# Sandwich layer on eight cores: the class part of the attention output is added in PSUM by TensorE, and VectorE gates the sum in one pass

## The chip, the cores and the metric

The kernel runs on the 8 cores of one Trainium2 chip. Each core computes 2048 of the 16384 tokens (2 sequences of 8192, four cores to a sequence) and loads 1536 tokens ahead of them as a halo. The metric is the device time in microseconds of the slowest core; lower is better. The cores exchange nothing.

## The reference

`x` has shape (2, 8192, 1024), with 16 heads of 64 columns. The layer is attention over 44 fixed offsets, gated, followed by a linear layer with a factored weight:

```python
# x = x + LN(attn(LN(x)));  x = x + LN(ffn(LN(x)))
OFFSETS = 0..32, 48, 64, 96, 128, 192, 256, 384, 512, 768, 1024, 1536
q, k, v = split(x @ qkv_w.T + qkv_b)                       # heads of 64
logit_o[n] = q[n].k[n-o] / 8 * (1 + q[n].scale_embed[o]) + pos_bias[o]
p = softmax over the 44 offsets (offsets beyond the start masked)
out[n] = sum_o p_o[n] * v[n-o];  out *= if_gain
gate = sigmoid(x @ gate_w.T + gate_b)
attn = (out * gate) @ out_w.T + out_b
ffn(x) = x @ W.T, W (1024 x 1024) built from G1_R, G2_R, G1_I, G2_I
```

## The kernel before

Offsets 0 to 32 and 48 are handled for blocks of 128 neighbouring tokens (the local part: "l"). The ten others offsets are handled for classes of tokens 32 apart (the class part: "c"). The last phase, which the change touches, starts when both parts have their softmax weights in two DRAM images (`plimg`, `pcimg`).

Before the last phase, `class_pv` has computed P.V of the class part for all tokens: 16 units, each evicted from PSUM by VectorE (L654, with the v bias added) into the tile `rk` at `CF`. It lies there feature-major as `[oc][class][token of the class]`, so that neighbouring tokens are 64 elements apart. The rest of `rk` holds the raw probabilities (`PR`), the sorted ones (`PH`) and v (`VB`).

The last phase is a software pipeline over 16 tiles of 128 tokens, written out by hand: step `s` (20 of them) issues parts of four tiles. In the order of the code, which is the order on each engine's queue (the tile in brackets):

1. SyncE loads the raw probabilities of tile s+3; TensorE transposes half of the sorted probabilities of tile s+1 (`p_turn`, L613) into bank 4, and ScalarE evicts them (L375); GpSimd sorts half of those of tile s+2 (`p_sort`, L376).
2. `d_fin1(s-3)`: VectorE takes the statistics of the second linear layer's result (L262, L263, L264), ScalarE the square root (L880).
3. `d_pv(s)`: 32 small matmuls of P.V of the local part (`pv_unit`, L627) into banks 5 and 6.
4. `d_merge(s)`: VectorE adds banks 5 and 6 and the class part, permuted back to token order, into the f16 tile `AT` (L818). It frees the banks.
5. `d_fin2(s-3)`: three operations of one element per partition on VectorE (L883, L884, L886).
6. `d_gate(s)`: VectorE multiplies `AT` by the gate (in `ry`) into `GA` (L826).
7. `d_op(s-1, 0)`: first half of the output projection on TensorE (`proj`: one matmul for the bias, L831, eight of 128x512, L834).
8. `d_tr(s-2)`: TensorE transposes the normalized tile (L864), ScalarE evicts it (L868).
9. The second half of `p_turn` (s+1) and `p_sort` (s+2), as in 1.
10. `d_fo(s-3)`: ScalarE normalizes the result of the second linear layer (L894, two halves), which frees the banks of `d_ffn`.
11. `d_op(s-1, 1)`, then `d_ln(s-1)`: VectorE statistics (L262, L263), residual (L852 twice), statistics again, with two square roots on ScalarE (L848, L856), and the normalization to f16 on ScalarE (L859).
12. Gate chunks (`g_next(3)`) as long as any are left, which is in the first steps only.
13. `d_ffn(s-2)`: the second linear layer, two times `proj`. It rotates through the same four banks as `d_op`, so that its banks are the ones that `d_fo(s-3)` frees.
14. `d_out(s-3)`: GpSimd adds (L902), SyncE stores.

Each engine takes its queue in order; a wait holds all that is behind it.

Of the kernel before, what the change touches and what calls it, by code (L numbers as in the profile page):

```python
# [12 lines left out]
ALU = mybir.AluOpType  # L13
# [3 lines left out]
TOK, HALO, TOT = 2048, 1536, 3584  # L17
NG = TOT // 512
NQ = TOK // 128
NU = 16  # L20
# [23 lines left out]
class Queues:  # L44
# [6 lines left out]
    def op(self, eng, fn, *waits, done=True):  # L51
        tok = None
        if done:
            self.count[eng] += 1
            tok = (eng, self.count[eng])
        self.q[eng].append((fn, waits, tok, 1))
        return tok
# [31 lines left out]
def sv(h, off, *dims, p0=0, np_=128):  # L89

    pitch = h.shape[1]
    return bass.AP(h, p0 * pitch + off, [[pitch, np_]] + [list(d) for d in dims])


def build_program():
# [28 lines left out]
    op, dma = qs_.op, qs_.dma  # L124

    def sb(name, cols, dtype=F16):
        return es.enter_context(nc.sbuf_tensor(name, [128, cols], dtype))

    rk = sb("rk", 8 * TOT)
    rq = sb("rq", 8 * TOK)  # L130
    ry = sb("ry", 5 * 4096)
    rw0, rw1, rw2 = sb("rw0", 8192), sb("rw1", 8192), sb("rw2", 8192)
# [4 lines left out]
    idb = sb("idb", 128)  # L137
# [6 lines left out]
    ps = es.enter_context(nc.psum_tensor("ps", [128, 4096], F32))  # L144
# [4 lines left out]
    bank = [None] * 8  # L149
# [57 lines left out]
    for name in ("plimg", "pcimg"):  # L207
        o = 0
        while o < PIMG:
            n = min(128 * 4096, PIMG - o) // 128  # L210
# [215 lines left out]
    for n, (chunk, g, oc) in enumerate(work):  # L426
        tt = 4 + n // 2
# [42 lines left out]
    s1done, pdone, scat = {}, {}, {}  # L470
# [106 lines left out]
    CF = 0  # L577
# [7 lines left out]
    def raw_load(U, *waits):  # L585
        s, kind, idx = U % 2, "cl"[U // NU], U % NU
        img = t["plimg"] if kind == "l" else t["pcimg"]
        for half in range(2):
            raw[U] = dma("sync", f"bp{s}", sv(rk, PR[s], [1, ROW], p0=half * 64, np_=64),
                         bass.AP(img, (idx * 128 + half * 64) * SKEW, [[ROW, 64], [1, ROW]]), *prfree[s], *waits)  # L590

    def v_load(U):
        s, kind, idx = U % 3, "cl"[U // NU], U % NU
        for half in range(2):
            if kind == "l":
                src = bass.AP(t["vimg"], (HALO + idx * 128 + half * 64 - 48) * D, [[D, WK], [1, D]])
            else:
                src = bass.AP(t["vimg"], (2 * idx + half) * D, [[32 * D, WK], [1, D]])
            vld[U] = dma("sync", f"bv{s}", sv(rk, VB[s] + half * 1024, [1, 1024], np_=WK), src, vbfree[s],
                         *(vdone[tt] for tt in range(NG * 4)))  # L600

    def p_sort(U, hh, eng):

        dst = sv(rk, PH + hh * 8 * WK, [WK, 8], [1, WK])
        src = sv(rk, PR[U % 2] + hh * 8, [1, 8], [16, WK])
        pcp[U, hh] = evict(eng, dst, src, raw[U], phfree[hh])
        if hh == 1:
            prfree[U % 2] = (pcp[U, 0], pcp[U, 1])

    def p_turn(U, hh, b, eng):  # L610

        for h in range(8):
            tp = op("tensor", lambda e, h=h: e.transpose(  # L613
                bass.AP(ph, b * 1024 + h * 128, [[8192, WK], [1, 128]]),
                sv(rk, PH + (hh * 8 + h) * WK, [1, WK]), idb[:]), pcp[U, hh], bank[b], done=(h == 7))
        phfree[hh] = tp
        bank[b] = ptt[U, hh] = evict(eng, PT[U % 2][0:WK, hh * 1024:(hh + 1) * 1024],
                                     bass.AP(ph, b * 1024, [[8192, WK], [1, 1024]]), tp, ptfree[U % 2])

    def pv_unit(U, b):  # L620

        s = U % 3
        for half in range(2):
            for hp in range(8):
                for r in range(2):
                    h = 2 * hp + r
                    mm = op("tensor", lambda e, h=h, hp=hp, r=r, half=half: e.matmul(  # L627
                        ps[r * 64:(r + 1) * 64, b * 512 + hp * 128 + half * 64:b * 512 + hp * 128 + half * 64 + 64],
                        sv(rk, VB[s] + half * 1024 + h * 64, [1, 64], np_=WK),
                        PT[U % 2][0:WK, h * 128 + half * 64:h * 128 + half * 64 + 64],  # L630
                        start=True, stop=True, tile_position=(0, r * 64)),
                        ptt[U, 0], ptt[U, 1], vld[U], bank[b], bank[b + 1], done=(hp == 7 and r == 1))
        vbfree[s] = ptfree[U % 2] = mm
        return mm
# [10 lines left out]
    cpart = {}  # L645
# [11 lines left out]
    gtok, thfree, gn = {}, [None, None], [0]  # L657
# [67 lines left out]
    for s in range(NB):  # L725
# [34 lines left out]
        else:  # L760
# [8 lines left out]
            U = w + 3  # L769
# [18 lines left out]
    smlast = pdone[NU - 1]  # L788


    FO = [rx[:, i * 1024:(i + 1) * 1024] for i in range(2)]
    AT = [rw1[:, i * 1024:(i + 1) * 1024] for i in range(2)]
    GA = [rw1[:, (2 + i) * 1024:(3 + i) * 1024] for i in range(2)]
    X2 = [rw1[:, (4 + i) * 1024:(5 + i) * 1024] for i in range(2)]
    XT = [rw1[:, (6 + i) * 1024:(7 + i) * 1024] for i in range(2)]
# [2 lines left out]
    pvm, gat, opm, x1t, c1t, x2t, x2f, ffm, aggt, xtt = ({} for _ in range(10))  # L798
# [12 lines left out]
    def d_pv(tt):  # L811
        pvm[tt] = pv_unit(NU + tt, 5)

    def d_merge(tt):
        src = sv(ps, 5 * 512, [128, 8], [32, 4], [1, 32])
        cin = sv(rk, CF + 4 * tt, [TOK, 8], [1, 4], [64, 32])
        at = AT[tt % 2].rearrange("p (a i c) -> p a i c", a=8, i=4)
        bank[5] = bank[6] = mrg[tt] = op("vector", lambda e: e.tensor_tensor(at, src, cin, ALU.add),  # L818
                                         pvm[tt], cpart[NU - 1], smlast)

    def d_gate(tt):
        g = 3 + tt // 4
        gsrc = sv(ry, gslot[g] * 4096 + (tt % 4) * 128, [512, 8], [1, 128])
        a2 = AT[tt % 2].rearrange("p (a n) -> p a n", a=8)
        go = GA[tt % 2].rearrange("p (a n) -> p a n", a=8)
        gat[tt] = op("vector", lambda e: e.tensor_tensor(go, a2, gsrc, ALU.mult), mrg[tt], gtok[g, 7], opm.get(tt - 2))  # L826

    def proj(src, w, wrow, half, *waits):
        b = pj_bank()
# [9 lines left out]
    def d_op(tt, half):  # L839
        opb[tt, half], opm[tt] = proj(GA[tt % 2], wo_, obr, half, gat[tt], wol)  # L840
# [21 lines left out]
    def d_tr(tt):  # L862
        for c in range(8):
            tp = op("tensor", lambda e, c=c: e.transpose(ph[:, 7 * 1024 + c * 128:7 * 1024 + (c + 1) * 128],  # L864
                                                         X2[tt % 2][:, c * 128:(c + 1) * 128], idb[:]),
                    x2t[tt], bank[7], done=(c == 7))
        x2f[tt] = tp
        bank[7] = xtt[tt] = op("scalar", lambda e: e.copy(XT[tt % 2], ph[:, 7168:8192]), tp, ffm.get(tt - 2))  # L868

    def d_ffn(tt):  # L870
        for half in range(2):
            ffb[tt, half], ffm[tt] = proj(XT[tt % 2], wbig, fbr, half, xtt[tt], wbl)
# [4 lines left out]
    def d_fin1(tt):  # L877
        src = ff_src(tt)
        a = stats(src[0], src[1], 32, ffm[tt])
        aggt[tt] = op("scalar", lambda e: e.activation(sc(46), sc(45), AF.Sqrt, bias=epsc), a)  # L880

    def d_fin2(tt):
        r = op("vector", lambda e: e.reciprocal(sc(46), sc(46)), aggt[tt])  # L883
        m = op("vector", lambda e: e.scalar_tensor_tensor(  # L884
            sc(47), sc(44), sc(46), sc(80 + tt % 4), ALU.mult, ALU.add), r)
        m = op("vector", lambda e: e.tensor_scalar(sc(47), sc(47), -1.0, None, ALU.mult), m)  # L886
        fom[tt] = m
# [6 lines left out]
                "scalar", lambda e, fo=fo, h=h: e.activation(fo, src[h], AF.Identity, bias=sc(47), scale=sc(46)),  # L894
                m, fofree[tt % 2])

    fofree, fot, mrg, fom = [pdone[NU - 1]] * 2, {}, {}, {}

    def d_out(tt):
        X = XS[tt % 4]  # L900
# [9 lines left out]
    for s in range(NQ + 4):  # L910
        old, tr, pj = (s - 3 if 0 <= s - 3 < NQ else None, s - 2 if 0 <= s - 2 < NQ else None,
                       s - 1 if 0 <= s - 1 < NQ else None)
        if s + 3 < NQ:
            raw_load(NU + s + 3)
        if s + 1 < NQ:
            p_turn(NU + s + 1, 0, 4, "scalar")
        if s + 2 < NQ:
            p_sort(NU + s + 2, 0, "gpsimd")
        if old is not None:
            d_fin1(old)  # L920
        if s < NQ:
            d_pv(s)
            if s + 3 < NQ:
                v_load(NU + s + 3)
            d_merge(s)
        if old is not None:
            d_fin2(old)
        if s < NQ:
            d_gate(s)
        if pj is not None:  # L930
            d_op(pj, 0)
        if tr is not None:
            d_tr(tr)
        if s + 1 < NQ:
            p_turn(NU + s + 1, 1, 4, "scalar")
        if s + 2 < NQ:
            p_sort(NU + s + 2, 1, "gpsimd")
        if old is not None:
            d_fo(old)
        if pj is not None:  # L940
            d_op(pj, 1)
        if pj is not None:
            d_ln(pj)
        g_next(3)
        if tr is not None:
            d_ffn(tr)
        if old is not None:
            d_out(old)
        if s >= 3:
            x_again(s + 1)  # L950
# [95 lines left out]
```

How the kernel before makes its waits and increments, by code:

```python
                def body(e, ops=self.q[eng]):  # L69
                    seen = {}
                    for fn, waits, tok, amount in ops:
                        for w in waits:
                            if w is not None and seen.get(w[0], 0) < w[1]:
                                e.wait_ge(sems[w[0]], w[1])
                                seen[w[0]] = w[1]
                        if fn is None:
                            continue
                        ins = fn(e)
                        if tok is not None:
                            ins.then_inc(sems[tok[0]], amount)
```

## Time and profile before

| | us |
|---|---|
| median of 3 runs | 731.53 (728.51 to 776.9) |
| the profiled execution | 731.03 |
| its span on the slowest core (core 0) | 729.1 |
| spans of the other cores | 719.3 to 728.6 |
| busy: TensorE, VectorE | 600.9 (82%), 431.9 (59%) |
| busy: ScalarE, GpSimd | 342.0 (47%), 272.9 (37%) |

The profiled execution took 1.9 us more than its span, before the first and after the last instruction. The shares are means over phases with different limits. The last phase is the stretch from about 498 us to the end.

### The profile page before, as it was taken

How to read it: one execution, taken by the hardware profiler on the slowest of the kernel's cores; microseconds unless marked ns; L12 is line 12 of the kernel's file. 1: busy time of each engine (PE TensorE's matmuls, PEld its weight loads, DVE VectorE, ACT ScalarE, POOL GpSimd, SP SyncE). 2: the span in 40 equal slices, each digit the busy share in tenths (PEclk: the TensorE clock that was granted, in tenths of full speed). 3: DMA queues.
4: the chain of work that ended last, by engine and by line, in shares of the span. 5: the costliest groups of instructions: out<-in, count | busy, mean ns of one | idle time of the engine just before them, and what ended most of it. 6: DMA issues, size and time to landing. Idle time of an engine off the chain costs nothing.

```text
span 729.1 us, 15108 instructions; the slowest of 8 cores (719.3 to 729.1 us)
## 1 busy us (share of the span) xinstructions
PE 600.9 (82%) x5408; PEld 312.8 (43%) x5408; DVE 431.9 (59%) x772; ACT 342.0 (47%) x480; POOL 272.9 (37%) x282
## 2 busy tenths in 40 slices
PE   1899969999989999999993496738788888888864
PEld 0444434444434555555541364535344444444431
DVE  4455555322232377788825367545458888888872
ACT  3566654333323655556531362624554545454532
POOL 3088888300000324332242445603424544445120
PEclk9999989999999999999996799857899999999996
DMA  8948997556575687898774988599314545553311
GB/s 211 237 151 224 281 272 249 181 178 204 127 147 161 186 204 209 202 245 207 184 173 75 164 205 208 151 247 248 89 51 127 172 146 170 150 167 106 116 58 58
DMA packets 73977, 126.49 MB, mean 173 GB/s; under 512 B 31116, under 2 KB 34316, under 8 KB 73392
## 3 DMA queue, kind: packets, MB, share of 16 engines
q1 hardware_dynamic: 51136, 71.06, 36.6%
q0 software_dynamic: 8608, 24.47, 17.1%
q10 hardware_dynamic: 14160, 30.00, 11.5%
q8 instruction: 44, 0.72, 0.4%
q14 instruction: 29, 0.24, 0.1%
HBM read 85.39 MB, written 50.59 MB: 187 GB/s over the span
## 4 chain that ended last, share of the span: by engine, by line
PE 46%; DVE 20%; DMA 9%; issue 8%; POOL 8%; ACT 5%; SPq 2%; DVEq 1%; ACTq 0%; POOLq 0%
PE ps L318 17%; PE ps L347 14%; PE ps L481 4%; DVE stt L262 4%; DVE stt L263 4%; PE ps L834 3%; DVE rq L852 3%; POOL rq L236 2%; DVE stt L884 2%; PE ps L499 2%; POOL rq L238 2%; SPq L62 2%; PE ps L613 2%; DMA simg<-rs 2%; DMA rk<-plimg 2%
## 5 line engine op out<-in xcount | busy, mean ns | idle before, releaser
L318 PE MATMUL ps<-ry,rw 128*128 128x512 f16 x832 | 194.6, 387 | 23.4 <-ACT rx L664 12.0
L318 PEld LDWEIGHTS ps<-ry,rw 128*128 128x128 f16 x832 | 79.2, 100 | 117.5 <-issue 33.2
L376 DVE CAST rs<-ps 128x896 f16<-128x896 f32 x32 | 34.7, 1090 | 81.1 <-PE ps L395 74.7
L613 PE MATMUL ps<-idb,rk 128*112 128x128 f16 x512 | 42.4, 236 | 41.8 <-DVE rk L376 25.1
L376 POOL COPY rk<-rk 128x896 f16<-128x896 f16 x28 | 50.3, 1804 | 70.2 <-PE ps L613 67.1
L347 PE MATMUL ps<-rw,ry 128*128 128x512 f16 x320 | 75.5, 380 | 0.0
L667 POOL TENSOR_SCALAR ry<-rx,cst 128x512 f16<-128x512 f32 x32 | 35.1, 1101 | 81.7 <-ACT rx L664 81.7
L834 PE MATMUL ps<-rw 128*128 128x512 f16 x256 | 63.0, 391 | 0.0
L834 PE MATMUL ps<-rq,rw 128*128 128x512 f16 x256 | 62.2, 387 | 0.0
L376 DVE COPY rk<-rk 128x896 f16<-128x896 f16 x36 | 35.5, 1027 | 43.0 <-DMA rk<-pcimg 22.3
L613 PEld LDWEIGHTS ps<-idb,rk 128*112 128x112 f16 x512 | 38.5, 144 | 51.8 <-issue 47.1
L352 ACT CAST rv<-ps 128x512 f16<-128x512 f32 x56 | 32.9, 587 | 55.7 <-PE ps L347 45.9
L327 ACT ACTIVATE rk<-ps,cst 128x512 f16<-128x512 f32 x56 | 38.1, 680 | 29.4 <-PE ps L318 29.3
L902 POOL TENSOR_TENSOR rq<-rq,rx 128x1024 f32<-128x1024 f32 x14 | 32.9, 2350 | 47.6 <-ACT rx L894 45.6
L62 POOL DMA_DIRECT2D rw<-cimg x32 | 16.7, 528 | 73.7 <-DMA cimg<-rs 73.5
L347 PEld LDWEIGHTS ps<-rw,ry 128*128 128x128 f16 x320 | 28.3, 98 | 36.7 <-issue 7.2
L236 POOL TENSOR_TENSOR rq<-rq 128x512 f32<-128x512 f32 x32 | 33.9, 1060 | 23.5 <-DMA rq<-g 20.0
L375 ACT COPY rv<-ps 112x1024 f16<-112x1024 f16 x32 | 31.4, 1013 | 23.4 <-PE ps L613 23.4
L334 ACT ACTIVATE rq<-ps,cst 128x512 f16<-128x512 f32 x32 | 21.7, 684 | 41.2 <-PE ps L318 34.9
L831 PE MATMUL ps<-rt,sel 128*128 128x512 f16 x64 | 25.1, 392 | 19.4 <-ACT rx L894 15.8
L664 ACT ACTIVATE rx<-ps,cst 128x512 f32<-128x512 f32 x32 | 21.7, 687 | 39.1 <-POOL ry L667 20.2
L834 PEld LDWEIGHTS ps<-rw 128*128 128x128 f16 x256 | 25.6, 100 | 30.5 <-issue 3.6
(109 smaller groups left out, 1024.6 us busy)
## 6 DMA issues: line engine op xcount, KB each, us to landing
rk<-vimg SPq DMA_DIRECT2D x64, 224.0 KB, 5.4
rx<-xs SPq DMA_DIRECT2D x18, 512.0 KB, 9.7
rq<-xs SPq DMA_DIRECT2D x16, 512.0 KB, 5.0
out<-rq SPq DMA_DIRECT2D x16, 512.0 KB, 2.7
plimg<-zt ACTq DMA_DIRECT2D x7, 1024.0 KB, 19.6
simg<-rs SPq DMA_DIRECT2D x32, 224.0 KB, 2.9
pcimg<-zt ACTq DMA_DIRECT2D x7, 1024.0 KB, 4.7
vimg<-rv ACTq DMA_DIRECT2D x28, 256.0 KB, 3.6
```

The costliest lines, as they stand in the source:

```text
L62: self.q[eng].append((lambda e: e.dma_start(out=out, in_=in_), waits, tok, 16))
L236: tk = op("gpsimd", lambda e, o_=dst, a_=a, b_=b: e.tensor_tensor(o_, a_, b_, ALU.mult), *gts[ri], tk)
L318: mm = op("tensor", lambda e, ic=ic, wof=wof: e.matmul(ps[:, b * 512:(b + 1) * 512], w[:, wof:wof + 128], yt[:, yo + ic * 512:yo + (ic + 1 ...
L327: kev[g, oc] = op("scalar", lambda e: e.activation(rk[:, oc * TOT + g * 512:oc * TOT + (g + 1) * 512], src, AF.Identity, bias=kbc[:, oc:oc ...
L347: mm = op("tensor", lambda e, ic=ic, yo=yo: e.matmul(src, yt[:, yo:yo + 128], rw0[:, half * 4096 + ic * 512:half * 4096 + (ic + 1) * 512], ...
L352: bank[b] = op("scalar", lambda e: e.copy(dst, src), mm, vst[s])
L375: return op("scalar", lambda e: e.copy(dst, src), *waits)
L376: return op(eng, lambda e: e.tensor_copy(dst, src), *waits)
L613: tp = op("tensor", lambda e, h=h: e.transpose(bass.AP(ph, b * 1024 + h * 128, [[8192, WK], [1, 128]]), sv(rk, PH + (hh * 8 + h) * WK, [1, ...
L667: gtok[g, oc] = thfree[s] = op("gpsimd", lambda e: e.tensor_scalar(dst, TH[s], hifg[:, oc:oc + 1], hifg[:, oc:oc + 1], ALU.mult, ALU.add), ...
L834: mm = op("tensor", lambda e, ic=ic: e.matmul(dst, src[:, ic * 128:(ic + 1) * 128], w[:, ic * 1024 + half * 512:ic * 1024 + (half + 1) * 512],
L902: lambda e: e.tensor_tensor(X, X, FO[tt % 2], ALU.add), fot[tt], x2t[tt])
```

## The change

For the tiles of the last phase, `pv_unit` first issues two identity matmuls (128x512, f16), one for each of the banks 5 and 6. They put the class part there in token order: the moving operand reads runs of 4 neighbouring elements of `rk`, the output is written 32 elements (128 bytes) apart. They start the accumulation, and the 32 matmuls of P.V add to it. `d_merge` and the tile `AT` go. `d_gate` multiplies the banks by the gate, straight from PSUM, and it frees the banks now, later in VectorE's order than `d_merge` did.

```diff
     def pv_unit(U, b):
         s = U % 3
+        if U >= NU:
+            for q in range(2):
+                op("tensor", lambda e, q=q: e.matmul(
+                    sv(ps, (b + q) * 512, [128, 4], [1, 32], [32, 4]), idb[:],
+                    sv(rk, CF + 4 * q * TOK + 4 * (U - NU), [TOK, 4], [64, 32], [1, 4]), start=True, stop=False),
+                    cpart[NU - 1], bank[b], bank[b + 1], done=False)
         for half in range(2):
...
-                        start=True, stop=True, tile_position=(0, r * 64)),
+                        start=(U < NU), stop=(U < NU or (half == 1 and hp % 4 == 3)), tile_position=(0, r * 64)),
...
-    AT = [rw1[:, i * 1024:(i + 1) * 1024] for i in range(2)]
...
-    def d_merge(tt):
-        src = sv(ps, 5 * 512, [128, 8], [32, 4], [1, 32])
-        cin = sv(rk, CF + 4 * tt, [TOK, 8], [1, 4], [64, 32])
-        at = AT[tt % 2].rearrange("p (a i c) -> p a i c", a=8, i=4)
-        bank[5] = bank[6] = mrg[tt] = op("vector", lambda e: e.tensor_tensor(at, src, cin, ALU.add),
-                                         pvm[tt], cpart[NU - 1], smlast)
-
     def d_gate(tt):
         g = 3 + tt // 4
+        src = sv(ps, 5 * 512, [128, 8], [1, 128])
         gsrc = sv(ry, gslot[g] * 4096 + (tt % 4) * 128, [512, 8], [1, 128])
-        a2 = AT[tt % 2].rearrange("p (a n) -> p a n", a=8)
         go = GA[tt % 2].rearrange("p (a n) -> p a n", a=8)
-        gat[tt] = op("vector", lambda e: e.tensor_tensor(go, a2, gsrc, ALU.mult), mrg[tt], gtok[g, 7], opm.get(tt - 2))
+        bank[5] = bank[6] = gat[tt] = op("vector", lambda e: e.tensor_tensor(go, src, gsrc, ALU.mult),
+                                         pvm[tt], gtok[g, 7], opm.get(tt - 2), smlast)
...
             d_pv(s)
             if s + 3 < NQ:
                 v_load(NU + s + 3)
-            d_merge(s)
```

## Rows read from the trace of the kernel before

**Rows 1.** Timeline of VectorE, core 0: start, length, engine, line, operation, tiles, shape.

```profile
616.86 1.89 DVE L818 TENSOR_TENSOR rw<-ps,rk 128x1024 f16<-128x1024 f32 x1
...
618.92 1.45 DVE L884 SCALAR_TENSOR_TENSOR stt<-stt 128x1 f32<-128x1 f32 x1
...
620.55 0.68 DVE L826 TENSOR_TENSOR rw<-rw,ry 128x1024 f16<-128x1024 f16 x1
621.15 0.69 DVE L262 BATCH_NORM_STATS2 stt<-ps 128x6 f32<-128x512 f32 x1
```

**Rows 2.** Timeline of VectorE: starts of `d_ln`; brackets: idle before, releaser.

```profile
547.61 0.69 DVE L262 BATCH_NORM_STATS2 stt<-ps 128x6 f32<-128x512 f32 x1
...
670.15 0.69 DVE L262 BATCH_NORM_STATS2 stt<-ps 128x6 f32<-128x512 f32 x1
...
681.71 0.70 DVE L262 BATCH_NORM_STATS2 stt<-ps 128x6 f32<-128x512 f32 x1 [0.47 <-PE ps L834]
...
692.73 0.69 DVE L262 BATCH_NORM_STATS2 stt<-ps 128x6 f32<-128x512 f32 x1
...
703.38 0.70 DVE L262 BATCH_NORM_STATS2 stt<-ps 128x6 f32<-128x512 f32 x1 [1.38 <-PE ps L834]
```

**Rows 3.** Timeline of ScalarE, the same step.

```profile
615.52 1.24 ACT L859 ACTIVATE rw<-rq,stt 128x1024 f16<-128x1024 f32 x1 [0.68 <-DVE stt L858]
616.66 0.99 ACT L375 COPY rv<-ps 112x1024 f16<-112x1024 f16 x1
617.56 0.29 ACT L880 ACTIVATE stt<-stt 128x1 f32<-128x1 f32 x1
...
618.65 1.02 ACT L375 COPY rv<-ps 112x1024 f16<-112x1024 f16 x1
620.79 1.45 ACT L894 ACTIVATE rx<-ps,stt 128x512 f32<-128x512 f32 x2 [1.12 <-DVE stt L886]
```

**Rows 4.** Timeline of TensorE, the same step, and one row of a later step.

```profile
617.80 0.62 PE L613 MATMUL ps<-idb,rk 128*112 128x128 f16 x8 [0.29 <-ACT rv L375]
...
618.48 1.89 PE L834 MATMUL ps<-rq,rw 128*128 128x512 f16 x8
621.71 0.38 PE L831 MATMUL ps<-rt,sel 128*128 128x512 f16 x1 [1.34 <-ACT rx L894]
...
625.59 0.61 PE L613 MATMUL ps<-idb,rk 128*112 128x128 f16 x8
...
626.76 0.39 PE L831 MATMUL ps<-rt,sel 128*128 128x512 f16 x1
...
679.72 1.89 PE L834 MATMUL ps<-rq,rw 128*128 128x512 f16 x8
```

**Rows 5.** Timeline of GpSimd, the same step.

```profile
618.56 1.80 POOL L376 COPY rk<-rk 128x896 f16<-128x896 f16 x1 [2.70 <-PE ps L613]
```

**Rows 6.** Lines L884 and L818: duration ns min/median/max, first and last start.

```profile
L884 DVE SCALAR_TENSOR_TENSOR stt<-stt x16: 219/1450/1742, 545.1 to 722.7; 128x1 f32<-128x1 f32 x16
...
L818 DVE TENSOR_TENSOR rw<-ps,rk x16: 1877/1894/1952, 499.5 to 689.7; 128x1024 f16<-128x1024 f32 x16
```

**Rows 7.** Groups by line and shape: VectorE reads PSUM without gaps (`class_pv`).

```profile
L654 DVE TENSOR_TENSOR rk<-ps,cst 128x1024 f16<-128x1024 f32 x16 | 19.4, 1215 | 0.0
```

**Rows 8.** Lines L395 (moving operand without gaps) and L481 (64 bytes apart): ns min/median/max.

```profile
L395 PE MATMUL ps<-rk,rq x512: 206/209/301, 113.8 to 228.8; 64*64 64x112 f16 x171
...
L481 PE MATMUL ps<-rk,rq x512: 363/384/481, 230.7 to 358.7; 64*64 64x112 f16 x171
```

**Rows 9.** Timeline of TensorE, first steps of the last phase.

```profile
498.24 1.06 PE L627 MATMUL ps<-rv,rk 112*64 112x64 f16 x32
499.55 1.07 PE L613 MATMUL ps<-idb,rk 128*112 128x128 f16 x8 [0.26 <-ACT rs L375]
...
506.32 0.69 PE L627 MATMUL ps<-rs,rk 112*64 112x64 f16 x32
...
525.49 1.07 PE L613 MATMUL ps<-idb,rk 128*112 128x128 f16 x8 [3.84 <-ACT rs L375]
```

More of the change, by code:

```diff
@@ L895, in d_fo @@
                 m, fofree[tt % 2])
-    fofree, fot, mrg, fom = [pdone[NU - 1]] * 2, {}, {}, {}
+    fofree, fot, fom = [pdone[NU - 1]] * 2, {}, {}
     def d_out(tt):
```

## The prediction, made before the changed kernel was run

> **What bounds the kernel now.** The page's busy shares say little: VectorE has 59% of the span, but only the last phase is touched. I read the chain that ended last there and then each engine's timeline. From 547.61 us on, `d_ln` starts at even distances: ten periods to 670.15, so 12.25 us each [rows 2]. In these steps its first operation at 621.15 has no idle time before it; it starts when L826 is through [rows 1, 2]. VectorE's queue sets the pace, while TensorE waits 1.34 us before L831 for the evictions L894 [rows 4]. VectorE's work in a period holds one oddity: L884 works on one element per partition and takes 1.45 us, in its shortest case 0.22 [rows 1, 6]. It starts at 618.92 and ends at 620.37; GpSimd's sort copy runs from 618.56 to 620.36 [rows 1, 5]. So L884 stands behind that copy.
>
> The next thing to read is what is late when VectorE isn't. Between 670.15 and 681.71 the period was 11.56 us, and there `d_ln` did wait 0.47 us, for TensorE [rows 2]. GpSimd had no more to sort in that step, L884 was short. The circle behind it, from the steady step: `d_ln` starts at T; L859 starts 6.61 later (615.52 against 621.15 less a period of 12.25); ScalarE then evicts the first transposes (L375), TensorE does the second (617.80), and the projection's eight matmuls start at 618.48, 2.96 after L859 [rows 3, 4]; VectorE takes them up 1.99 after their start (679.72 to 681.71) [rows 2, 4]. 6.61 + 2.96 + 1.99 = 11.56. No step of this circle is touched by the change. In the steady step the same sum gives 620.47 for what starts at 621.15: only **0.68 us** of a period hangs on VectorE's queue.
>
> **Part 1, merge and gate become one.** Removed: 1.89 (L818) and 0.68 (L826) [rows 1]. Added: one pass over 1024 elements that reads PSUM without gaps. The nearest row is L654, 1.22 us for the same size [rows 7]; the other end is 1.9, what L818 takes with gaps in both inputs [rows 6]. I take 1.22: of the two inputs neither has gaps now inside 128 elements. Busy time saved: 1.35 us.
>
> **Part 2, L884 moves ahead of the sort copy.** Without the merge, `d_fin2` waits for the root L880. Count from L859's start: L880 starts at 2.04, `d_ln`'s successor statistics being done earlier; root 0.29, one short VectorE operation and two hand-overs of about 0.1 (an estimate from the 0.22 of the shortest L884) bring L884 to about 2.7, its end to 2.9. The second transposes start at 2.28 and the sort copy at 3.04 [rows 3 to 6]. So L884 is short, and another 1.2 us go. Then the gate starts at about 3.1 and ends at 4.3; `d_ln` is due at 4.95. VectorE is no longer late, with 0.6 us to spare; a gate of 1.9 us would end at 5.0 and cost next to nothing in steady steps.
>
> The Trainium skill (SBUF — State Buffer, Who interferes with whom) says that a VectorE instruction with two SBUF inputs contends with a GpSimd instruction that reads SBUF, the later one blocks fully, and one with at most one SBUF input doesn't contend. The trace agrees for L884 (1.45 beside the copy, 0.22 without). By the rule the new gate, with one input in PSUM, is safe beside the copy though the copy runs during all of it, and L826 was not; were it wrong the sum would be that of the second rival.
>
> **Part 3, two identity matmuls of 512 columns on TensorE.** No row writes PSUM with gaps. Lower end: a 512-column matmul takes 0.215 (eight of them and the bias 1.94, half of the 3.88 from 621.71 to 625.59) [rows 4], so 0.43 for two. Upper end: L481 reads its 112 columns with 64-byte gaps and takes 384 ns against L395's 209, 1.56 ns more per column [rows 8]; on top of 0.42 that is 1.0 us for 512 columns and 2.03 for two. Less than 0.43 is excluded, since the columns must stream. I take 0.43, since the shape is that of L831 and L834 and the reads are runs of four; both ends stay.
>
> Is it hidden? TensorE's work in a period is 3.88 (second layer), 1.17 (transposes and P.V), 1.94 (projection), twice 0.46 (617.80 to 618.48 less one matmul) and 1.94 again, 9.85 in all [rows 4]. Now from T: L859 of the step before the next starts at 6.61, the second evict of L375 at 9.75, L894 behind it at 10.7 (earlier than now, since L884 is), the second layer 0.92 later at 11.6; transposes and P.V follow at 15.5, the projection at 16.7, the two blocks of transposes at 18.6 and 19.1, and the eight matmuls could start at 19.8. The circle wants them at 11.56 + 6.61 + 2.96 = 21.1. So **1.3 us of slack** cover the identity matmuls; at 2.03 they cost 0.7 a period, which is just what the circle gave. If that cover were gone they would cost 0.43 a step.
>
> The Trainium skill (Advanced Engine Details and Errata, PSUM Cachelines) speaks against this part: any access pattern of PSUM with gaps significantly slows matmuls, two neighbouring elements should be contiguous. It names no factor, and no matmul of this trace shows it. At half speed it would be 0.86 for two, still inside the slack, and the sum would be 0.4 higher from the first steps alone.
>
> **Part 4, banks 5 and 6 come free later.** They are freed by the gate at about T + 10.9 instead of the merge; the next identity matmuls come at T + 16. Cost nothing; the cover is 5 us. The added wait on the class part has been met since before the phase, and P.V accumulates at the same rate as L834 does.
>
> **Part 5, the first steps, where nothing hides it.** P.V of tile 0 runs before the clock has risen (1.06 against 0.69 us) [rows 9]; there the two cost twice 0.43, less the 0.26 that the next transposes wait anyway: 0.6. P.V of tile 1 at 506.32 lies on the chain, back to back with its neighbours: 0.43. In the step of tile 3 (541 to 548 us) the first L884, 545.1, waits for a double sort copy, 1.74 us [rows 6]; its root is late because ScalarE loads a table, so it stays behind the copy. The gate that follows it is on the chain and is 0.54 longer than L826: 0.54. Sum: +1.6.
>
> **The sum.** Ten periods at 0.69: −6.9. The period 681.71 to 692.73 (11.02) shrinks to that of 692.73 to 703.38 (10.65), where there is no merge: −0.4 [rows 2]. First steps: +1.6. In all −5.7, so 731.03 − 5.7 = 725.3. The profiled execution is 0.5 under the median, well inside the spread of the runs, so I give **725.5**.
>
> **The rivals.** *First, the clock.* At 525.49 TensorE has waited 3.84 us and takes 1.07 for what takes 0.61 at full clock [rows 4, 9]. The identity matmuls fill 0.43 of this wait. If the clock then stays up, transposes and projection run 0.46 + 1.94 sooner: 723. Against it: 3.4 us of waiting remain.
>
> *Second, the new order on VectorE meets the copy after all; slower.* L884 starts 0.3 us ahead of the sort copy by the sum in part 2, and this is the point from which it decides: if L884 comes at or behind 3.04 after L859, it waits for the copy's end at 4.84, and the gate, now 1.22 instead of 0.68, ends near 6.15 where `d_ln` is due at 4.95. The period is then 11.56 + 1.2 = 12.76, worse than before by 0.51: +5.1, with the first steps +1.6 and the end −0.4: 737. The same follows if it is the gate that the copy blocks. For it: the narrow 0.3. Against it: both start from the same eviction L375, so the order repeats, and L818, also with one input in PSUM, never took over 1.95 [rows 6].
>
> *Third, identity matmuls at the upper end.* Steady steps gain nothing (12.2 against 12.25); tile 0 costs about 2.03 − 0.26 = 1.8, tile 1 2.0, the gate of tile 3 0.5, the end −0.4: +4, so 735.
>
> *Fourth,* something I can't see makes the circle no shorter, and only the first steps' costs and nothing else stay: 731 to 733.
>
> **Chances.** Forecast 0.55 (own range 723 to 728); clock 0.12; copy 0.10; slow identity matmuls 0.13; no gain 0.07; 0.03 for anything else. The range 721 to 735.5 leaves out the copy case and half of what is odd. Two per cent are 14.6 us (716.9 and 746.2), about what a measurement of this kernel can tell from no change; no case above reaches either. Faster by over 2% would need the circle itself shorter, 0.04; slower, the copy case with slow identity matmuls, 0.04.
>
> **What would show it.** Right: `d_ln` starts 11.56 apart with a short wait for L834 before it; L884 near 0.22 in the steady steps; the new gate at 1.2; the two new matmuls about 0.45 together; the 1.34 before L831 mostly gone; P.V waits for no bank. Wrong: L884 still at 1.45 or the gate above 2 (copy); new matmuls above 0.7 each with the waits for L859 gone (slow writes); or a releaser before `d_ln` that isn't TensorE.

## The result and the profile after

| | before | after |
|---|---|---|
| median, 5 runs each | 728.51 us | 723.47 us |
| profiled execution | 731.03 us | 721.81 us |
| its span | 729.1 us | 719.5 us |

The ratio of after to before is **0.9907, with a 95% interval of 0.9883 to 0.9931**: 6.8 us of 728.5, faster, though by less than two per cent. (Both kernels had a run in which the cores of a die were slowed, 776.9 and 746.1; the ratio leaves such runs out.) The medians differ by 5.0 us and the profiled executions by 9.2; the ratio is the measure that I go by. The page of the profile after begins so, busy microseconds and shares by engine:

```profile
span 719.5 us, 15152 instructions; the slowest of 8 cores (712.5 to 719.5 us)
...
PE 612.2 (85%) x5440; PEld 313.8 (44%) x5440; DVE 403.7 (56%) x756; ACT 341.1 (47%) x480; POOL 271.2 (38%) x282
```

VectorE has 28 us less to do, and 7 us or so arrive. VectorE's timeline in a steady step of the changed kernel, the counterpart of [rows 1, 2] (L825 is the new gate):

```profile
624.61 0.16 DVE L883 RECIPROCAL stt<-stt 128x1 f32<-128x1 f32 x1 [1.01 <-ACT stt L880]
624.88 0.22 DVE L884 SCALAR_TENSOR_TENSOR stt<-stt 128x1 f32<-128x1 f32 x1
...
625.31 1.22 DVE L825 TENSOR_TENSOR rw<-ps,ry 128x1024 f16<-128x1024 f32 x1
627.13 0.70 DVE L262 BATCH_NORM_STATS2 stt<-ps 128x6 f32<-128x512 f32 x1 [0.60 <-PE ps L834]
```

L884 takes 0.22 instead of 1.45, the gate 1.22, and `d_ln` waits 0.60 for TensorE where it did not wait before. The 1.01 before L883 is VectorE waiting for the root L880, which the merge used to fill. GpSimd's sort copy, the counterpart of [rows 5], starts 0.34 behind L884 and runs through the whole gate:

```profile
625.22 1.82 POOL L376 COPY rk<-rk 128x896 f16<-128x896 f16 x1 [3.22 <-PE ps L613]
```

TensorE in the same step (compare [rows 4]; L626 are the identity matmuls, L634 is P.V):

```profile
615.58 0.38 PE L831 MATMUL ps<-rt,sel 128*128 128x512 f16 x1
...
619.46 0.61 PE L613 MATMUL ps<-idb,rk 128*112 128x128 f16 x8
619.90 1.02 PE L626 MATMUL ps<-rk,idb 128*128 128x512 f16 x2
620.86 0.69 PE L634 MATMUL ps<-rv,rk 112*64 112x64 f16 x32
...
623.56 0.61 PE L864 MATMUL ps<-idb,rw 128*128 128x128 f16 x8
624.46 0.62 PE L613 MATMUL ps<-idb,rk 128*112 128x128 f16 x8 [0.29 <-ACT rs L375]
```

The wait of 1.34 us before L831 is down to 0.13 (the eight matmuls ahead of it run from 613.56 to 615.45). From 619.90 to 620.86 the pair holds TensorE 0.96 us, twice the 0.43 that two matmuls of the projection take. Last, where the time went, from the starts of `d_ln` on VectorE:

```profile
546.14 0.69 DVE L262 BATCH_NORM_STATS2 stt<-ps 128x6 f32<-128x512 f32 x1
...
661.84 0.70 DVE L262 BATCH_NORM_STATS2 stt<-ps 128x6 f32<-128x512 f32 x1 [0.59 <-PE ps L834]
...
673.41 0.70 DVE L262 BATCH_NORM_STATS2 stt<-ps 128x6 f32<-128x512 f32 x1 [0.41 <-PE ps L834]
684.07 0.70 DVE L262 BATCH_NORM_STATS2 stt<-ps 128x6 f32<-128x512 f32 x1 [0.20 <-PE ps L834]
694.73 0.70 DVE L262 BATCH_NORM_STATS2 stt<-ps 128x6 f32<-128x512 f32 x1 [1.38 <-PE ps L834]
```

The ten periods took 115.70 instead of 122.54: 11.57 each, −6.84. The next three took 32.89 instead of 33.23 [rows 2]: −0.34. After the last `d_ln` 24.77 us remain instead of 25.72: −0.95. What is left of the 9.6 us between the spans is −1.47 before the third `d_ln`; the phase already began 1.9 us earlier, by differences of the earlier phases, whose code is the same in both kernels, so the first steps lost 0.4.

Core 0 is one of eight, and at both ends of the phase it is not typical. The medians over the eight cores of the same two executions, in us:

| stretch | before | after | difference | core 0 |
|---|---|---|---|---|
| last class part (L654, after: L661) to first `d_ln` | 16.28 | 17.84 | +1.56 | +2.17 |
| first to second `d_ln` | 18.25 | 16.59 | −1.66 | −2.34 |
| second to third `d_ln` | 17.12 | 17.69 | +0.57 | +0.58 |
| ten periods | 122.55 | 115.70 | −6.85 | −6.84 |
| next three periods | 33.23 | 32.89 | −0.34 | −0.34 |
| last `d_ln` to the end | 24.90 | 24.82 | −0.08 | −0.95 |

The differences add up to −6.8, which is also what the ratio gives. The −0.95 at the end belongs to core 0 alone: before the change the last half of its second linear layer ran partly at the lower clock (2.77 us), after it at full clock (1.89), as on six of the seven other cores before.

### The profile page after: what moved, and what is told of

It is laid out like the page before. It is cut to its first block, busy times and chain, and to the rows that moved or that the text cites. A ratio compares the mean times of both kernels' runs of the same rounds, so it can differ in the third digit from the quotient of the medians.

```text
span 719.5 us, 15152 instructions; the slowest of 8 cores (712.5 to 719.5 us)
## 1 busy us (share of the span) xinstructions
PE 612.2 (85%) x5440; PEld 313.8 (44%) x5440; DVE 403.7 (56%) x756; ACT 341.1 (47%) x480; POOL 271.2 (38%) x282
## 4 chain that ended last, share of the span: by engine, by line
PE 52%; DVE 15%; DMA 9%; issue 8%; POOL 7%; ACT 6%; SPq 2%; DVEq 0%; ACTq 0%; POOLq 0%
PE ps L318 19%; PE ps L347 14%; PE ps L834 5%; PE ps L481 4%; DVE stt L262 4%; DVE stt L263 3%; DVE rq L852 3%; PE ps L613 3%; PE ps L499 2%; SPq L62 2%; DMA simg<-rs 2%; POOL rq L236 2%; DMA rk<-plimg 2%; POOL rq L238 2%; DMA rk<-pcimg 2%
## 5 line engine op out<-in xcount | busy, mean ns | idle before, releaser
L318 PE MATMUL ps<-ry,rw 128*128 128x512 f16 x832 | 196.4, 390 | 24.7 <-ACT rx L671 12.1
L674 POOL TENSOR_SCALAR ry<-rx,cst 128x512 f16<-128x512 f32 x32 | 33.4, 1047 | 84.9 <-ACT rx L671 84.8
L834 PE MATMUL ps<-rq,rw 128*128 128x512 f16 x256 | 60.5, 379 | 0.0
L376 DVE COPY rk<-rk 128x896 f16<-128x896 f16 x36 | 38.3, 1107 | 38.6 <-DMA rk<-pcimg 15.8
L902 POOL TENSOR_TENSOR rq<-rq,rx 128x1024 f32<-128x1024 f32 x14 | 32.9, 2348 | 35.5 <-ACT rx L894 34.7
L375 ACT COPY rv<-ps 112x1024 f16<-112x1024 f16 x32 | 31.4, 1013 | 23.9 <-PE ps L613 23.9
L834 PEld LDWEIGHTS ps<-rq,rw 128*128 128x128 f16 x256 | 25.1, 98 | 26.5
```

Source lines behind the costliest of these rows:

```text
L318: mm = op("tensor", lambda e, ic=ic, wof=wof: e.matmul(ps[:, b * 512:(b + 1) * 512], w[:, wof:wof + 128], yt[:, yo + ic * 512:yo + (ic + 1 ...
L375: return op("scalar", lambda e: e.copy(dst, src), *waits)
L376: return op(eng, lambda e: e.tensor_copy(dst, src), *waits)
L674: gtok[g, oc] = thfree[s] = op("gpsimd", lambda e: e.tensor_scalar(dst, TH[s], hifg[:, oc:oc + 1], hifg[:, oc:oc + 1], ALU.mult, ALU.add), ...
L834: mm = op("tensor", lambda e, ic=ic: e.matmul(dst, src[:, ic * 128:(ic + 1) * 128], w[:, ic * 1024 + half * 512:ic * 1024 + (half + 1) * 512],
L902: lambda e: e.tensor_tensor(X, X, FO[tt % 2], ALU.add), fot[tt], x2t[tt])
```

## The experiments

Ratios are to the kernel before on the same chip. The lines of the changed kernel keep their numbers except where an edit moves them.

**Is the gain L884 alone?** The kernel before, with `d_fin2` ahead of `d_merge`:

```diff
-            d_merge(s)
         if old is not None:
             d_fin2(old)
         if s < NQ:
+            d_merge(s)
             d_gate(s)
```

> The kernel before with one swap in VectorE's order: d_fin2 (L883, L884, L886) ahead of d_merge, so that L884 comes before GpSimd's second sort copy. VectorE's work stays otherwise. Theory (the merge filled the wait for the root L880, and what counts is when VectorE is through): L884 takes 0.22, but VectorE now waits some 1.0 us for the root, the merge runs from 3.1 to 4.9 and the gate to 5.55 after L859, where d_ln could start at 4.95: period 12.16 against 12.25, total within 2 us of the kernel before, ratio 0.998 to 1.002. Rival (the gain of the change came from freeing L884, 1.2 us a period): period about 11.6, ratio near 0.99.

Measured: **745.85 us, ratio 1.019 (1.0149 to 1.0231)**. L884 takes 0.22 in all steps but that of tile 3, and the kernel is slower by 14 us. The rival falls at once; but my own number, no change, is as wrong. The profile (VectorE, then TensorE 6 us later) shows one thing at first sight:

```profile
645.31 1.79 DVE L854 TENSOR_TENSOR stt<-stt 128x1 f32<-128x1 f32 x1
```
```profile
651.06 1.01 PE L864 MATMUL ps<-idb,rw 128*128 128x128 f16 x8 [3.25 <-ACT rw L859]
```

L854, also one element with two inputs in SBUF, stands behind a GpSimd copy inside `d_ln` in three of the 16 steps (0.15 in the others), and TensorE's transposes after a wait of 3.25 us run at half clock. I took that for the cause and tested it, with L854 written as

```diff
-        op("vector", lambda e: e.tensor_tensor(c1, sc(12), sc(14), ALU.mult), done=False)
+        op("vector", lambda e: e.tensor_scalar(c1, sc(12), sc(14), None, ALU.mult), done=False)
```

> The kernel before with d_fin2 ahead of d_merge, as in the run that came out 14 us slower, and L854 as tensor_scalar. Theory (the swap let L854, which stands inside the circle, wait up to 1.8 us for a GpSimd operation, and the longer stalls cost TensorE its clock on top): with L854 freed the period is the 12.16 that was forecast for the swap alone, ratio 0.998 to 1.002. Rival (the swap itself costs, by the order merge, gate and statistics on VectorE): the ratio stays at 1.01 or more.

Measured: **744.56 us, ratio 1.0215 (1.0174 to 1.0256)**. L854 took 0.20 to 0.21 in all 16 cases and nothing was won: that theory fell, the rival stands. VectorE, the step of tile 3 and a steady step:

```profile
546.05 2.61 DVE L826 TENSOR_TENSOR rw<-rw,ry 128x1024 f16<-128x1024 f16 x1
...
573.42 0.69 DVE L262 BATCH_NORM_STATS2 stt<-ps 128x6 f32<-128x512 f32 x1
...
583.16 2.05 DVE L818 TENSOR_TENSOR rw<-ps,rk 128x1024 f16<-128x1024 f32 x1
585.31 0.69 DVE L826 TENSOR_TENSOR rw<-rw,ry 128x1024 f16<-128x1024 f16 x1
586.59 0.70 DVE L262 BATCH_NORM_STATS2 stt<-ps 128x6 f32<-128x512 f32 x1 [0.58 <-PE ps L834]
```

and TensorE in that step:

```profile
581.41 0.61 PE L864 MATMUL ps<-idb,rw 128*128 128x128 f16 x8 [1.62 <-ACT rw L859]
...
582.99 3.49 PE L834 MATMUL ps<-rq,rw 128*128 128x512 f16 x8
```

Three things add up. The merge no longer fills the wait for the root L880; it takes 2.05 instead of 1.89, and L826, which reads what it wrote, starts 2.15 behind its start, where the next operation came 1.81 behind it before. So the period is 12.4 to 12.5 rather than 12.16. In the step of tile 3 L826 takes 2.61 instead of 0.68, beside GpSimd's L902 (545.77 to 548.12). And in some steps the projection runs below full clock (3.49 us for what takes 1.89) after TensorE's waits; such a period is 13.17 to 13.25. How much of the 16 us each has I did not separate. What is settled is that freeing L884 in this order, without taking work from VectorE, gains nothing.

**Is VectorE's work in slack, and does an operation with two SBUF inputs wait?** The gate in two passes:

```diff
-        bank[5] = bank[6] = gat[tt] = op("vector", lambda e: e.tensor_tensor(go, src, gsrc, ALU.mult),
-                                         pvm[tt], gtok[g, 7], opm.get(tt - 2), smlast)
...
+        bank[5] = bank[6] = mrg[tt] = op("vector", lambda e: e.tensor_copy(AT[tt % 2], src), pvm[tt], smlast)
...
+        gat[tt] = op("vector", lambda e: e.tensor_tensor(go, a2, gsrc, ALU.mult), mrg[tt], gtok[g, 7], opm.get(tt - 2))
```

> The changed kernel, but the gate is made of two passes on VectorE again: a copy of banks 5 and 6 to AT (PSUM to f16), then AT times the gate, both inputs in SBUF. Theory (an operation with two SBUF inputs waits for a running GpSimd copy): the second pass is ready at about 4.2 after L859, the sort copy runs to 4.84, so it ends near 5.5 and d_ln, due at 4.95, is late by 0.55: period 12.1, about 5 us over the changed kernel, ratio to the kernel before 0.997. Rival (no such blocking; only work counts): the two passes end at 4.9, period stays 11.57, d_ln has next to no wait left, ratio 0.991 to 0.992.

Measured: **729.34 us, ratio 0.9977 (0.9953 to 1.0001)**. GpSimd's copy, and the second pass (L829) with the next `d_ln` behind it:

```profile
617.98 1.82 POOL L376 COPY rk<-rk 128x896 f16<-128x896 f16 x1 [3.55 <-PE ps L613]
```
```profile
619.40 0.95 DVE L829 TENSOR_TENSOR rw<-rw,ry 128x1024 f16<-128x1024 f16 x1
620.27 0.68 DVE L262 BATCH_NORM_STATS2 stt<-ps 128x6 f32<-128x512 f32 x1
```

The copy ends at 619.80. L829 ends at 620.35, 0.55 later, and took 0.27 more than the 0.68 of the same pass in [rows 1]; the copy still ran for 0.40 of it. In the tiles in which no copy ran beside it L829 took 0.69; in the first, where the copy still ran for 1.24, it took 1.79. So it waits for the copy's end, less some 0.13 us. The total is as forecast, the period 11.93 instead of 11.57 where 12.1 was forecast. So the new gate's 0.6 us of slack is real, and what goes beyond it is paid. About 0.27 of the 0.36 us is the copy's by these rows, the rest the second pass itself.

**How much slack has TensorE?** The pair issued twice:

```diff
-            for q in range(2):
+            for rep, q in ((0, 0), (0, 1), (1, 0), (1, 1)):
...
-                    ..., start=True, stop=False),
+                    ..., start=True, stop=(rep == 0)),
```

> The changed kernel with the pair of identity matmuls issued twice for each tile; the second pair overwrites the first, so the result is the same. A pair took 0.95 us from start to start in the changed kernel, and TensorE's waits there leave about 0.55 before the second transposes. Theory (TensorE has that slack and no more): the period grows by 0.95 less 0.55, to about 11.95; with tiles 0 and 1 in full, +7 us over the changed kernel, ratio near 1.000. Rival A (the identity matmuls are fully covered): period 11.57, ratio 0.993. Rival B (TensorE already sets the pace): period 12.5, ratio 1.01.

Measured: **734.25 us, ratio 1.0057 (1.0031 to 1.0083)**. TensorE, and VectorE's `d_ln`:

```profile
614.34 1.88 PE L626 MATMUL ps<-rk,idb 128*128 128x512 f16 x4
616.15 0.70 PE L634 MATMUL ps<-rs,rk 112*64 112x64 f16 x32
```
```profile
609.67 0.70 DVE L262 BATCH_NORM_STATS2 stt<-ps 128x6 f32<-128x512 f32 x1 [1.13 <-PE ps L834]
...
621.84 0.70 DVE L262 BATCH_NORM_STATS2 stt<-ps 128x6 f32<-128x512 f32 x1 [1.20 <-PE ps L834]
```

The two pairs take 1.81, 0.85 more; the period is 12.17, 0.60 more. So 0.25 of slack was left beside one pair of 0.96, 1.2 in all. The prediction had 1.3; the expectation of this run had 0.55 left beside the pair, which was too much, and the result lies between its theory and its rival B.

**What makes the pair slow, the read or the write?** First a form with the same result: read single elements 128 bytes apart, write without gaps.

```diff
-                    sv(ps, (b + q) * 512, [128, 4], [1, 32], [32, 4]), idb[:],
-                    sv(rk, CF + 4 * q * TOK + 4 * (U - NU), [TOK, 4], [64, 32], [1, 4]), ...
+                    sv(ps, (b + q) * 512, [1, 512]), idb[:],
+                    sv(rk, CF + 4 * q * TOK + 4 * (U - NU), [TOK, 4], [1, 4], [64, 32]), ...
```

> The changed kernel, but the identity matmuls read element by element with gaps of 128 bytes and write PSUM without gaps; the result is the same. Theory A (a read of single elements 128 bytes apart costs what L481 shows, 2.0 ns a column, and more than the gapped write): the pair takes 2.0 us, 1.1 more than now, the period about 12.3, ratio 1.01. Theory B (it is the gapped write of PSUM that makes the pair take 0.95; a gapped read is no worse): the pair takes 0.95 or less, ratio 0.991.

Measured: **732.52 us, ratio 1.0039 (1.0017 to 1.0061)**. The pair and P.V behind it:

```profile
601.62 1.87 PE L626 MATMUL ps<-rk,idb 128*128 128x512 f16 x2
603.42 0.69 PE L634 MATMUL ps<-rv,rk 112*64 112x64 f16 x32
```

The pair takes 1.80 from start to start (1.76 ns a column), the period is again 12.17: theory A, a little milder than forecast. Then three looks at forms that put the class part elsewhere, each read from one execution.

> The changed kernel with identity matmuls that read 512 neighbouring elements of rk and write 512 neighbouring columns of PSUM; the class part lands at other tokens than in the reference. This prices the shape alone: a pair should take 0.43 us from start to start, as L831 and L834 do, if gaps are all that makes it 0.95. Rival: the identity matmuls cost more than their columns for another reason (a bank that P.V wrote, the load of the identity), and the pair stays above 0.8. The total should lie at or just under that of the changed kernel, since TensorE has slack.

> The changed kernel with identity matmuls that read 512 neighbouring elements and write PSUM 128 bytes apart as now; the class part lands at other tokens than in the reference. Theory (the write is what costs: single columns in PSUM at half rate, 0.83 ns each): the pair takes 0.86 to 0.95. Rival (the reading of runs of four costs): 0.43.

> The changed kernel with identity matmuls that read runs of four elements 128 bytes apart as now and write PSUM without gaps; the class part lands at other columns of the same tokens' tile than in the reference. The counterpart of the run with gapped writes. If the write costs, the pair takes 0.43 here. If the read costs, 0.95: by single elements 128 bytes apart the pair took 1.80, which is 1.76 ns an element, and one such step for each run of four would be 0.45 a pair, hidden or not.

Without any gaps: 726.0 us. With gapped writes alone: 723.1. With runs of four read and writes without gaps: 723.2. Single executions do not rank such totals; what counts is the pairs, in this order:

```profile
610.99 0.59 PE L626 MATMUL ps<-rk,idb 128*128 128x512 f16 x2
...
611.51 0.66 PE L634 MATMUL ps<-rs,rk 112*64 112x64 f16 x30
```
```profile
608.09 1.02 PE L626 MATMUL ps<-rk,idb 128*128 128x512 f16 x2
609.04 0.69 PE L634 MATMUL ps<-rs,rk 112*64 112x64 f16 x32
```
```profile
609.90 0.60 PE L626 MATMUL ps<-rk,idb 128*128 128x512 f16 x2
610.42 0.70 PE L634 MATMUL ps<-rs,rk 112*64 112x64 f16 x32
```

0.52, 0.95, 0.52: reading runs of four costs nothing, **writing PSUM 128 bytes apart costs all of it**. Steady periods are 11.57 in all three, as in the changed kernel, since 0.43 us lie inside the slack. These looks show a second thing. TensorE before the second output projection, changed kernel first, then the form without gaps:

```profile
525.77 0.62 PE L613 MATMUL ps<-idb,rk 128*112 128x128 f16 x8 [2.99 <-ACT rs L375]
```
```profile
526.08 1.07 PE L613 MATMUL ps<-idb,rk 128*112 128x128 f16 x8 [3.41 <-ACT rs L375]
```

The slow pair fills more of this wait, and on this core the clock stays up; with the fast pair, as in the kernel before (3.84 us) [rows 9], it falls to half. But one core per run misleads here. In the form with gapped writes, on its slowest core, the wait was 2.98 and the transposes still ran full, yet the projection right behind them did not (1.89 at full clock):

```profile
524.88 3.25 PE L834 MATMUL ps<-rq,rw 128*128 128x512 f16 x8
```

All eight cores of every profiled run that keeps the second transposes in this place, by the length of this wait, and on how many cores the transposes or the projection behind it ran below full clock:

| wait, us | runs | cores below full clock |
|---|---|---|
| 3.84 | before, and the two with the swap | 24 of 24 |
| 3.41 | no gaps; runs of four | 14 of 16 |
| 2.98 | changed kernel, two-pass gate, gapped writes | 8 of 24 |
| 2.12 | pair twice; single elements read | 4 of 16 |

Where it stayed full, the first two `d_ln` lie 16.6 us apart, where it fell 17.6 to 18.95. So the slow pair makes the fall rarer, it does not exclude it. In the four runs below that move the transposes, TensorE waits at most 1.2 us here, and the clock falls on none of 32 cores.

**Is the circle what I took it for?** The second transposes leave it, on the changed kernel:

```diff
-        if s + 1 < NQ:
-            p_turn(NU + s + 1, 1, 4, "scalar")
-        if s + 2 < NQ:
-            p_sort(NU + s + 2, 1, "gpsimd")
         if old is not None:
             d_fo(old)
         if pj is not None:
             d_op(pj, 1)
+        if s + 1 < NQ:
+            p_turn(NU + s + 1, 1, 4, "scalar")
+        if s + 2 < NQ:
+            p_sort(NU + s + 2, 1, "gpsimd")
```

> The changed kernel with the second half of p_turn and of p_sort moved behind the second half of the output projection, on TensorE, ScalarE and GpSimd. Theory (the period is the circle d_ln, L859, eviction L375, transposes, projection): without eviction and transposes in it the circle is 10.65, as between the last tiles, and TensorE's work of 9.85 + 0.95 = 10.8 comes next: period 10.8 to 11.0, total 6 to 8 us under the changed kernel, ratio 0.980 to 0.983. Rival (the sort copy now pushes L902 later, and L854, which has two SBUF inputs, waits for L902 inside d_ln): L854 takes about 1 us, the circle is 11.5 again, ratio 0.990.

Measured: **715.26 us, ratio 0.9779 (0.9753 to 0.9806)**. GpSimd, then VectorE:

```profile
611.68 2.35 POOL L902 TENSOR_TENSOR rq<-rq,rx 128x1024 f32<-128x1024 f32 x1
```
```profile
609.68 0.69 DVE L262 BATCH_NORM_STATS2 stt<-ps 128x6 f32<-128x512 f32 x1
...
613.43 0.63 DVE L854 TENSOR_TENSOR stt<-stt 128x1 f32<-128x1 f32 x1
...
620.90 0.69 DVE L262 BATCH_NORM_STATS2 stt<-ps 128x6 f32<-128x512 f32 x1
```

The period is 11.22, more than the 10.8 to 11.0 that was forecast, and the total less than forecast. Both mechanisms are there: the circle is shorter, and L854 waits for the end of L902 at 614.03. `d_ln` no longer waits for TensorE: it starts when the gate is through, 4.27 after L859 starts (616.63). So the pace has moved to another circle, `d_ln`, L859, the eviction L375, the root L880, `d_fin2`, the gate. The periods give 3.5 us over ten; more came from the first steps, where the second transposes no longer hold up the projection: the first two `d_ln` lie 13.50 us apart instead of 16.60, the next two 16.64 instead of 17.69. With both one-element operations as `tensor_scalar`:

> The changed kernel with the second transposes and sort behind the projection, and with L854 and L884 written as tensor_scalar with two one-element scalar operands, so that neither has a second tensor input in SBUF. Theory (in the run with the late transposes L854 waited some 0.45 us a period for a GpSimd operation because of its second SBUF input): L854 takes 0.2, the period falls from 11.23 to 10.8 or 10.9, the total by 3 to 4 us more, ratio 0.973. Rival (the form of the operation makes no difference, any one-element operation waits for a running GpSimd one): L854 stays at 0.56 to 0.63, ratio 0.978.

Measured: **711.99 us, ratio 0.9799 (0.9749 to 0.9849)**. That is short of the 0.973 expected, and the ratios do not tell it from the run before it; the rows do:

```profile
609.92 2.35 POOL L902 TENSOR_TENSOR rq<-rq,rx 128x1024 f32<-128x1024 f32 x1
```
```profile
607.97 0.69 DVE L262 BATCH_NORM_STATS2 stt<-ps 128x6 f32<-128x512 f32 x1
611.72 0.20 DVE L854 TENSOR_SCALAR stt<-stt 128x1 f32<-128x1 f32 x1
...
618.91 0.69 DVE L262 BATCH_NORM_STATS2 stt<-ps 128x6 f32<-128x512 f32 x1
```

L854 runs in 0.20 in the middle of L902, and the period is 10.94: 6.61 from `d_ln` to L859, and 4.33 from there through the root and the gate to the next `d_ln`. The same order and forms on the kernel before, merge and all:

> The kernel before, merge on VectorE and all, with the late transposes and sort and with L854 and L884 as tensor_scalar: what the changed kernel gets in the run beside it, without the change itself. VectorE: the merge fills the wait for the root, L884 no longer waits for the copy, the gate ends 4.4 to 4.5 after L859, then 6.6 of d_ln: period 11.0 to 11.1 against 10.9. Theory (what the change gives hangs on the order around it; in the mended order VectorE has room for the merge): ratio 0.976 to 0.980, within 3 us of the same order with the change. Rival (VectorE's 1.35 us of work a period count in full): period 12.1, ratio 0.99.

Measured: **714.93 us, ratio 0.9816 (0.9759 to 0.9874)**, period 11.25 (549.97 to 628.74 in seven), VectorE never waiting for TensorE there; forecast were 11.0 to 11.1 and at most 0.980. By the periods the change is worth 0.3 us each in this order and 0.68 in its own; the totals of the two runs are not told apart. Last, the root L880 ahead of the first eviction:

> The kernel with the late transposes and the two tensor_scalar forms, and d_fin1 ahead of the first half of p_turn as well, so that ScalarE takes the root L880 before it evicts the first transposes. In the run without this step d_ln started when VectorE was through with the gate, 4.3 us after L859, and the root waited 0.6 of it behind the eviction. Theory: the gate ends 0.6 earlier, the circle is 10.65 and TensorE's 10.8 a period sets the pace: period 10.8 against 10.94, 1.4 us in all, ratio 0.975 to 0.979. Rival (the eviction, now 0.3 later, holds something else): period 11.0 or more.

Measured: **711.63 us, ratio 0.9752 (0.9703 to 0.9801)**, the lowest time in this study, though in totals not told apart from the last two on the changed kernel. `d_ln` starts:

```profile
594.49 0.70 DVE L262 BATCH_NORM_STATS2 stt<-ps 128x6 f32<-128x512 f32 x1
...
637.65 0.70 DVE L262 BATCH_NORM_STATS2 stt<-ps 128x6 f32<-128x512 f32 x1
```

10.79 a period over four of them, with waits of 0.37 and 0.20 for TensorE before the two between 600 and 620 us, while TensorE's rows between 594 and 627 us have no gap over 0.2 us: now TensorE's own 10.8 of work sets the pace, as expected.

## Why the prediction was right, step by step

**The sum (right, in part by luck).** Forecast were −5.7 us and a time of 725.5; measured were −6.8 by the ratio and a median of 723.47. The steady steps are right as forecast. In the first steps two errors, the price of the pair and the clock, nearly cancel.

**The circle (right).** 11.56 a period was forecast from one step of the old trace where VectorE had to wait; 11.57 was measured, −6.84 against −6.9. Moving two members out of the circle shortened the period at once, from 11.57 to 11.22, until another circle was the longest; so this one is shown and not only read.

**Part 1 (right).** The gate takes 1.22, the value of L654. The 0.6 of slack forecast behind it is the 0.60 that `d_ln` waits, and the two-pass run shows that it was all there was.

**Part 2 (right as to the order).** L884 starts 0.34 ahead of the copy, 0.3 was forecast. The gate runs beside the copy unharmed, as the Trainium skill (SBUF — State Buffer, Who interferes with whom) says of an operation with one SBUF input; the trace agrees, with 1.224 to 1.227 us for all 16 gates, 12 of which met a copy. Freeing L884 was no gain of its own, and the two runs with the swap show that my model of VectorE's order was good for the change and not for the swap. What a blocked L884 would have cost the changed kernel, the second rival's +1.2 a period, no run tested.

**Part 3 (mechanism right, size off).** The term mis-sized is the pair: 0.43 taken, 0.95 measured. The Trainium skill (Advanced Engine Details and Errata, PSUM Cachelines) says that access to PSUM with gaps slows matmuls, and names no factor; the trace agrees, 0.95 with gapped writes against 0.52 without, and the 0.86 that I had as an estimate at half speed was near. I should have taken it for the sum. It cost nothing in steady steps because of the 1.2 us of slack, forecast as 1.3.

**Part 4 (right).** In a steady step the next identity matmuls start 4.9 us after the gate's end (5 us was forecast), and no wait stands before any of the 32.

**Part 5 and the first rival (two errors that cancel).** The starts of the first two `d_ln`, before and after:

```profile
511.56 0.70 DVE L262 BATCH_NORM_STATS2 stt<-ps 128x6 f32<-128x512 f32 x1 [1.71 <-PE ps L834]
530.50 0.70 DVE L262 BATCH_NORM_STATS2 stt<-ps 128x6 f32<-128x512 f32 x1 [8.49 <-PE ps L834]
```
```profile
511.85 0.70 DVE L262 BATCH_NORM_STATS2 stt<-ps 128x6 f32<-128x512 f32 x1 [3.21 <-PE ps L834]
528.45 0.70 DVE L262 BATCH_NORM_STATS2 stt<-ps 128x6 f32<-128x512 f32 x1 [6.82 <-PE ps L834]
```

The first steps were to cost 1.6. From VectorE's last class part to the first `d_ln` it was 17.86 us instead of 15.69 on core 0, 2.2 more where 1.0 was forecast (1.6 more by the medians of the cores); the slow pair can account for it, since at the lower clock of tile 0 it took 1.84 (0.86 forecast) and in tile 1 0.95 (0.43 forecast). The gate of tile 3 cost 0.58, 0.54 forecast. But the clock rival, given 0.12, came true beside the forecast: 18.94 us between the first two `d_ln` became 16.60, −2.3 on core 0 and −1.7 by the medians. The table of waits shows that the slow pair did most of it: where the pair was fast the clock fell on 14 of 16 cores, where it was slow on 8 of 24. So I should have tied the two: a slower pair leaves a shorter wait. Both together, +0.4 on core 0 and +0.5 by the medians, where +1.6 was forecast. That leaves the total near the rival's 723, and that it is also near the forecast is luck.

## What to carry to other kernels

Look for the circle before counting work: one step of the old trace in which the busy engine did wait gave the new period to 0.01 us, where VectorE's saved work (28 us busy) would have promised four times the gain. Keep small operations with two tensor inputs in SBUF away from a running GpSimd operation; where one input is a single element, `tensor_scalar` does the same work, and L854 in that form did not wait. When the pace has moved to a circle, take links out of it: moving eight transposes and their eviction took the changed kernel from 0.991 to 0.978, though about half of that came in the first steps. And where the clock can fall, read all eight cores before calling a difference of one core an effect.

## What the runs showed of the hardware

- Identity matmuls of 128x512 that write PSUM in columns 128 bytes apart take 0.475 us each from start to start, without gaps 0.26 (pair with what follows it, 0.52); reads of single f16 elements 128 bytes apart take 0.90, reads of runs of four 0.26.
- A one-element VectorE operation with two SBUF inputs took up to 1.79 us beside a GpSimd copy (0.15 without). As `tensor_scalar` with one-element scalars L854 took 0.20 to 0.21 in all 16 cases, 11 of them inside GpSimd's L902, and L884 0.27; L884 in that form met a GpSimd operation only once, in the last run, and took 0.27 there too.
- A gate of 128x1024 with one input in PSUM and one in SBUF took 1.22 to 1.23 us with or without a GpSimd copy beside it.
- TensorE's clock at the same place of the program (before the second projection): behind a wait of 3.84 us the transposes or the projection ran at the lower level (1.2 GHz instead of 2.4) on 24 of 24 cores, behind 3.41 on 14 of 16, behind 2.98 on 8 of 24, behind 2.12 on 4 of 16. It cost 1.0 to 2.4 us.
